# 16-head attention with the keys on the partitions: scores come transposed from the matmul, and VectorE casts the latent keys' exponentials

## The chip, the cores and the metric

The kernel runs on one core of one Trainium2 chip. A core has TensorE (PE in the profile, its weight loads PEld), VectorE (DVE), ScalarE (ACT), GpSimd (POOL) and SyncE (SP), which run their own queues and wait for each other through semaphores. SBUF is the working memory, PSUM (eight banks of 128 x 512 f32) takes what TensorE computes. The metric is the device time of one execution in microseconds (us); smaller is better.

## The reference

The program computes four residual blocks on x of 4 batches x 256 tokens x 128 channels. Only the third one is touched in its arithmetic:

```python
# first stage: gated mLSTM cross attention over ctx, second stage: 8-head attention with 5 experts, fourth: 8-expert MLP
x = x + jnp.tanh(g_xattn[1]) * _L1_xattn_ref(ctx_1024, mask_BxS2_bf1, _layernorm(x, axis=-1), ...)   # the third stage
...
def _L1_xattn_ref(features, masks, latents, gm, bm, gl, bl, Wq, Wk, Wv, Wo):     # HEADS = 16, DIM_HEAD = 64, b = 4
    x = _layernorm(features, gm, bm)              # 256 keys from the features
    lat = _layernorm(latents, gl, bl)             # 256 queries, and 256 more keys
    q = (lat @ Wq).reshape(b, q_len, HEADS, DIM_HEAD).transpose(0, 2, 1, 3)
    kv_input = jnp.concatenate([x, lat], axis=1)
    kv_mask = jnp.concatenate([masks, jnp.ones((b, q_len), dtype=bool)], axis=1)
    ...                                           # k, v = kv_input @ Wk, @ Wv; q = q * SCALE
    sim = jnp.einsum('bhqd,bhfd->bhqf', q, k)
    sim = sim - jax.lax.stop_gradient(jnp.max(sim, axis=-1, keepdims=True))
    sim = jnp.where(kv_mask, sim, -jnp.inf)
    alphas = jax.nn.softmax(sim, axis=-1)
    out = jnp.einsum('bhqf,bhfd->bhqd', alphas, v)
    return out.transpose(0, 2, 1, 3).reshape(b, q_len, INNER) @ Wo
```

## The kernel before

The four blocks run one after the other as four stages. Every product that matters is made in three f16 matmuls: each f32 operand is split into a high f16 half and a low f16 half (the rest), and high x high, high x low and low x high are accumulated (`three`, L949).

**The third stage** (`pe_c`, `act_c`, `dve_c`) works through 4 batches x 16 heads x 2 tiles of 128 queries, 128 units of one tile of scores, 128 queries x 512 keys. The work is software-pipelined by `step(b, t)`, written out by hand for 32 units of a batch, with the middle in a hardware loop; queues are in order, so this text sets the order of the work. A unit goes through these stations:

- `scores` (L977): three matmuls of 64 rows x 512 columns, queries on the partitions.
- DVE at L1196: one pass over the bank that adds the mask, writes the negated scaled scores `sm` to SBUF, and takes the row's minimum (the softmax maximum).
- ACT at L1109: exp of `sm` with that maximum as bias, to `Pr` (f32).
- PE at L1029: four f32 transposes, so that the keys come to the partitions, which the product with V needs.
- ACT at L1102 copies the transposed tile to f16 (`PTh`), DVE at L1204 subtracts it from the bank (`PTl`).
- PE at L1016 to L1018: 12 matmuls of 65 columns with V (the 65th column is one, it gives the denominator).
- DVE at L1214 and L1218, once for four units: reciprocal of the denominators, and the product.

Beside that run the projections (`project`: K and V in three matmuls of 512 columns, Q of 256; ACT copies the high half, L1089, DVE subtracts it, L1174), and for every batch four transposes of the attention's output (`turn_ao`) and two f32 output projections (`project_ao`, L998).

**The second stage** ends in `dve_b` with two normalisations of the latents (L685), ten products (L769), a sum, and the split of the latents (`latent_split`, L691 and L693); its queries' path is on DVE and PE. `split` (L1596, L1598) turns a chunk of 1024 weight columns into two f16 halves on POOL; before, the eight chunks of the fourth stage's weights are split in `pool_c`, in the first units of the third stage.

## Time and profile before

| | |
|---|---|
| median of 3 runs | 800.03 us (799.91 to 800.35) |
| span of the profiled execution | 798.0 us |
| busy share PE, DVE, ACT, POOL | 82%, 80%, 45%, 34% |
| third stage, 393.5 to 687 us | 293.5 us: PE busy 285.8, DVE 243.0, ACT 207.1, POOL 28.8 |
| end of the second stage, 353 to 393.5 us | 40.5 us: PE busy 16.3, DVE 31.1, ACT 7.7, POOL 10.1 |

The span runs from the first to the last instruction of the profiled execution; a run's time holds some 2 us more around it. A busy share is an average over stages that have different limits, so the stage's own rows count. In a timeline a row gives the start, the duration, and what ended the idle time before it; since instructions of one engine overlap, what a row of work costs in a dense stretch is the distance between two starts, not its duration.

### The profile page before, as it was taken

To read this page: it belongs to the slowest core of one execution; us is meant where nothing else is said; L and a number is where in the kernel's file an instruction comes from. 1 tells how busy PE (TensorE), PEld (TensorE's weight loads), DVE (VectorE), ACT (ScalarE), POOL (GpSimd) and SP (SyncE) were. 2 spreads that over 40 slices of the span, in tenths; PEclk is the share of its full clock that TensorE was granted. 3 is DMA by queue.
4 is the path that set the end of the run, shared out by engine and by line. 5 is a ranking of instruction groups with operands and counts; after the bars stand their busy time and mean duration, and the time that the engine had idled before them with its cause. 6 is when DMAs were issued, how large, how long until landed. Compare 5 with 4: busy or idle time off the path is not lost. (4 is left out here: it accounts for less than half of the span.)

```text
span 798.0 us, 16645 instructions
## 1 busy us (share of the span) xinstructions
PE 651.7 (82%) x5465; PEld 405.4 (51%) x5465; DVE 635.4 (80%) x1391; ACT 355.3 (45%) x657; POOL 272.4 (34%) x253
## 2 busy tenths in 40 slices
PE   6499757797488388472589999999999999889997
PEld 5376511443254154252245556655655665557675
DVE  5747899579869969959489887888688879478887
ACT  2432200421231141131257777677677757546652
POOL 4433355146537727664058000000000000046663
PEclk9999968689599689665599999999999999989999
DMA  6211000000000000020013000000000000000000
GB/s 200 67 33 54 28 0 0 1 1 1 0 1 0 0 0 0 0 79 0 1 40 95 1 2 2 1 0 0 0 0 0 0 1 2 1 1 0 0 0 27
DMA packets 13111, 12.75 MB, mean 16 GB/s; under 512 B 2080, under 2 KB 10896, under 8 KB 13072
## 3 DMA queue, kind: packets, MB, share of 16 engines
q1 hardware_dynamic: 13072, 12.25, 5.2%
q8 instruction: 22, 0.36, 0.2%
q14 instruction: 17, 0.14, 0.1%
HBM read 11.72 MB, written 0.52 MB: 15 GB/s over the span
## 5 line engine op out<-in xcount | busy, mean ns | idle before, releaser
L1632 PE MATMUL bank<-ident,work 128*128 128x128 f32 x788 | 127.5, 292 | 8.9 <-DVE work L1832 3.0
L1632 PEld LDWEIGHTS bank<-ident,work 128*128 128x128 f32 x788 | 98.2, 151 | 29.2 <-issue 6.2
L1204 DVE TENSOR_TENSOR PTl<-bank,PTh 128x512 f16<-128x512 f32 x128 | 87.7, 685 | 28.2 <-ACT PTh L1102 27.7
L1567 POOL TENSOR_SCALAR rs<-mv 128x2 f32<-128x2 f32 (+2 forms) x12 | 2.4, 198 | 311.6 <-DVE mv L1775 311.6
L1109 ACT ACTIVATE work<-sm,nm 128x512 f32<-128x512 f32 x128 | 92.0, 719 | 10.9 <-DVE nm L1196 9.7
L1196 DVE CUSTOM_DVE_ANT_0 sm<-bank,maskrow 128x512 f32<-128x512 f32 x128 | 87.2, 681 | 7.1 <-ACT work L1109 5.7
L711 DVE TENSOR_TENSOR work<-bank,gatev 128x512 f32<-128x512 f32 x120 | 79.0, 682 | 14.5 <-PE bank L464 14.1
L1102 ACT ACTIVATE PTh<-bank 128x512 f16<-128x512 f32 x128 | 76.1, 594 | 29.0 <-PE bank L1632 26.7
L462 PE MATMUL bank<-weights,xbTh 128*128 128x512 f16 x120 | 49.4, 412 | 29.1 <-DVE work L711 27.2
L1016 PEld LDWEIGHTS bank<-work,PTh 128*128 128x128 f16 x512 | 46.0, 97 | 52.8 <-issue 47.1
L1328 DVE TENSOR_TENSOR work<-work 128x512 f16<-128x512 f32 x64 | 57.1, 949 | 13.0 <-POOL work L1390 13.0
L1390 POOL TENSOR_SCALAR work<-work 128x512 f16<-128x512 f32 x64 | 53.0, 851 | 36.6 <-ACT work L1322 34.0
L1016 PE MATMUL bank<-work,PTh 128*128 128x65 f16 x512 | 61.2, 196 | 2.1 <-DVE PTl L1204 2.1
L1017 PE MATMUL bank<-work,PTh 128*128 128x65 f16 x512 | 60.2, 195 | 0.0
L487 PE MATMUL bank<-kTh,qTh 64*128 64x256 f16 x64 | 21.3, 347 | 47.5 <-ACT work L628 38.4
L1018 PE MATMUL bank<-work,PTl 128*128 128x65 f16 x512 | 59.6, 193 | 0.0
L628 ACT ACTIVATE work<-bank,nm 128x256 f32<-128x256 f32 x64 | 26.7, 472 | 63.0 <-DVE nm L736 63.0
L951 PE MATMUL bank<-k2h,q2h 64*128 64x512 f16 x128 | 49.5, 387 | 3.3 <-DVE q2l L1174 2.1
L839 POOL TENSOR_TENSOR work<-work 128x512 f32<-128x512 f32 x24 | 30.5, 1270 | 63.2 <-DVE work L711 60.9
L464 PE MATMUL bank<-weights,xbTl 128*128 128x512 f16 x120 | 49.3, 411 | 0.0
L463 PE MATMUL bank<-weights,xbTh 128*128 128x512 f16 x120 | 49.2, 410 | 0.0
L953 PE MATMUL bank<-k2h,q2l 64*128 64x512 f16 x128 | 48.2, 376 | 0.0
(269 smaller groups left out, 1804.7 us busy)
## 6 DMA issues: line engine op xcount, KB each, us to landing
stage<-in_L_ffn_w SPq DMA_DIRECT2D x8, 512.0 KB, 3.8
stage<-in_L_ffn_Wkv SPq DMA_DIRECT2D x4, 640.0 KB, 4.0
stage<-in_L_ffn_Wq SPq DMA_DIRECT2D x2, 640.0 KB, 4.8
xt<-in_x SPq DMA_DIRECT2D x1, 512.0 KB, 4.1
ct<-in_ctx SPq DMA_DIRECT2D x1, 512.0 KB, 5.4
wo<-in_L_xattn_Wo SPq DMA_DIRECT2D x1, 512.0 KB
stage<-in_L_xattn_Wv SPq DMA_DIRECT2D x1, 512.0 KB, 3.4
stage<-in_L_xattn_Wq SPq DMA_DIRECT2D x1, 512.0 KB, 3.4
```

Source lines behind the costliest of these rows:

```text
L711: dve.tensor_tensor(heads8(m.prod[:, k, e, :]), heads8(bank_pj[c % 2][:, :]), wide(g, DH1), ALU.mult).then_inc(s.prod_ready, 1)
L951: pe.matmul(o, ah, bh, start=True, stop=False)
L1016: pe.matmul(o, ph, vh, start=(j == 0), stop=False)
L1017: pe.matmul(o, ph, vl, start=False, stop=False)
L1018: ins = pe.matmul(o, pl, vh, start=False, stop=(j == KT - 1))
L1102: act.activation(m.PTh[:, u % 2, :, :].rearrange("p n c -> p (n c)"), bank_T[use % 2][:, :], ACT.Copy).then_inc(s.c_T_hi, 1)
L1109: act.activation(m.Pr[:, t % 2, :], m.sm[:, t % 2, :], ACT.Exp, scale=-1.0, bias=m.nm[:, t % 4, 0:1]).then_inc(s.c_exp_done, 1)
L1196: dve.tensor_tensor_reduce(m.sm[:, t % 2, :], bank_S[t % 2][:, :], m.maskrow[:, :], -(DH2 ** -0.5), 3e38, ALU.add, ALU.min, m.nm[:, t % 4, ...
L1204: dve.tensor_tensor(m.PTl[:, u % 2, :, :].rearrange("p n c -> p (n c)"), bank_T[use % 2][:, :], m.PTh[:, u % 2, :, :].rearrange("p n c -> ...
L1328: dve.tensor_tensor(m.hTl[:, a, f, :], m.hf[:, use % HR, :], m.hTh[:, a, f, :], ALU.subtract).then_inc(s.h_lo, 1)
L1390: pool.tensor_scalar(m.hTh[:, use // FT, use % FT, :], m.hf[:, use % HR, :], 1.0, 0.0, ALU.mult, ALU.add).then_inc(s.h_hi, 1)
L1632: return pe.transpose(dst, src, m.ident[0:src.shape[0], 0:src.shape[0]])
```

## The change

The third stage is written anew. A step now is a pair of heads with all 256 queries, 32 steps in all, in this order on PE (`step`): transposed scores of the feature keys (`scores_T(t, 0)`), the row maximum's scores for the next pair's first query tile (`row_max(t + 1, 0)`), a projection or a transpose (job c), transposed scores of the latent keys, `row_max(t + 1, 1)`, the K projection (job f), the product with V of the pair before (`values`), the V projection (job h).

- `scores_T` computes the scores with the keys on the partitions: per half 12 matmuls of 64 rows x 256 columns that alternate between the two heads (rows 0 to 63 and 64 to 127, and two banks), and then subtracts the row maxima by a product of ones with a diagonal matrix of the maxima (`diag`, bf16), two matmuls of 512 columns. The f32 transposes of the exponentials are gone.
- `row_max` computes the scores a second time, from the high halves alone, queries on the partitions, only for their maximum: two matmuls of 512 columns and two of 256 with the mask row. DVE takes the maximum of 1024 columns (`take_max`) and writes `diag` (`spread_max`), twice a step.
- ACT takes exp straight from the banks. For the two tiles of feature keys it does so twice, f32 (`Pf`) and f16 (`Ph`); for the latent keys once, f32, and DVE casts that to f16 (`high_latents`, 128 x 1024). POOL subtracts (`low_exps`).
- The maxima's banks are bk[6] and bk[7]; `values` writes bk[6] too, and `project_ao` bk[7].
- Four of the eight weight splits are moved from the third stage into the last batch of the second; the other four stay at the start of `pool_c`. `turn_ao`'s copies move from ACT to DVE. Names have moved: L1174 is now L1248 to L1253, L1214 and L1218 are L1281 and L1285, L1598 is L1708.

The core of the diff, lines added:

```diff
+                    for k in range(2):
+                        latent_rstd(k)
+                        split(N_W1 + 2 + k)
...
-            for n in range(N_W0, N_W1):
+            for n in range(N_W0, N_W1 + 2):
+                if n == N_W1:
+                    pool.wait_ge(s.pj_ready, B * X1)
...
+            def step(it, t):
+                jobs, b, n = c_jobs(t), t // HP2, t % HP2
+                scores_T(it, t, 0)
+                if t + 1 < STEPS_C:
+                    row_max(it, t + 1, 0)
+                if "c" in jobs:
+                    job(it, (t, "c"), jobs["c"])
+                scores_T(it, t, 1)
+                if t + 1 < STEPS_C:
+                    row_max(it, t + 1, 1)
+                if "f" in jobs:
+                    job(it, (t, "f"), jobs["f"])
+                if t >= 1:
+                    values(it, t - 1, t)
+                if b >= 1 and n in (2, 4):
+                    project_ao(it, n // 2 - 1, job_no[t - 1, "c"], bank_wo)
+                if "h" in jobs:
+                    job(it, (t, "h"), jobs["h"])
...
+            def row_max(it, p, i):
+                if i == 0:
+                    pe.wait_ge(s.c_pj_free, it * PJ + (k_no[p] + 1))
+                    pe.wait_ge(s.maskrow_ready, it + (p // HP2 + 1))
+                    if p >= 3:
+                        pe.wait_ge(s.c_O_free, it * HP2 + (p - 2))
+                    elif p >= 1:
+                        pe.wait_ge(s.c_max_done, 2 * p)
                 else:
+                    pe.wait_ge(s.c_max_done, it * PAIRS + (2 * p + 1))
+                for h in range(2):
+                    r = slice(DH2 * h, DH2 * h + DH2)
+                    pe.matmul(bank_rm[h][:, :], m.q2h[r, p % 4, i * P:(i + 1) * P], m.k2h[r, p % 2, :], start=True, stop=False)
+                for h in range(2):
+                    r = slice(DH2 * h, DH2 * h + DH2)
+                    ins = pe.matmul(bank_rm[h][:, 0:S], m.first_row[r, :], m.maskrow[r, :], start=False, stop=True)
+                ins.then_inc(s.c_M_ready, 1)
...
+            def scores_T(it, p, half):
+                if p >= 1:
+                    pe.wait_ge(s.c_exp_done, it * EXPS + (3 * (p - 1) + 2 + half))
+                pair = bank_kq[2 * half:2 * half + 2]
+                for k in range(2):
+                    kt = 2 * half + k
+                    for x in range(3):
+                        for h in range(2):
+                            r = slice(DH2 * h, DH2 * h + DH2)
+                            key = (m.k2h, m.k2l, m.k2h)[x][r, p % 2, kt * P:(kt + 1) * P]
+                            q = (m.q2h, m.q2h, m.q2l)[x][r, p % 4, :]
+                            pe.matmul(pair[h][:, k * S:(k + 1) * S], key, q, start=(k == 0 and x == 0), stop=False)
+                if half == 0:
+                    pe.wait_ge(s.c_D_ready, it * PAIRS + (2 * p + 2))
+                for h in range(2):
+                    less = m.diag[:, p % 2, h * S:(h + 1) * S].unsqueeze(1).to_broadcast([P, 2, S])
+                    ins = pe.matmul(pair[h][:, :].rearrange("p (k c) -> p k c", k=2), m.onesb[:, :], less, start=False, stop=True)
+                ins.then_inc(s.c_S_ready, 1)
...
+            def values(it, p, t):
+                pe.wait_ge(s.c_P_lo, it * EXPS + (3 * p + 3))
+                if t < STEPS_C - 1:
+                    pe.wait_ge(s.c_max_done, it * PAIRS + (2 * t + 4))
+                else:
+                    pe.wait_ge(s.c_O_free, p)
+                if p % 4 == 0:
+                    pe.wait_ge(s.c_pj_free, it * PJ + (v_no[p // 4] + 1))
+                for u in range(4):
+                    o = bank_out[:, u * (DH2 + 1):(u + 1) * (DH2 + 1)]
+                    head = 2 * (p % HP2) + u // 2
+                    for kt in range(KT):
+                        ph, pl = (x[:, p % 2, kt, u * P:(u + 1) * P] for x in (m.Ph, m.Pl))
+                        vh, vl = (v[:, kt, head, :] for v in (m.v2h, m.v2l))
+                        pe.matmul(o, ph, vh, start=(kt == 0), stop=False)
+                        pe.matmul(o, ph, vl, start=False, stop=False)
+                        ins = pe.matmul(o, pl, vh, start=False, stop=(kt == KT - 1))
+                ins.then_inc(s.c_O_ready, 1)
...
+            def exps(it, p, r):
+                act.wait_ge(s.c_S_ready, it * PAIRS + (2 * p + r // 2 + 1))
+                if p >= 1:
+                    act.wait_ge(s.c_P_lo, it * EXPS + (3 * (p - 1) + r + 1))
+                if r == 0 and p % HP2 == 0:
+                    act.wait_ge(s.maskbias_ready, it + (p // HP2 + 1))
+                if r < 2:
+                    src, bias = banks[:, 2:4, r * S:(r + 1) * S], m.maskbias[:, r:r + 1]
+                    hi, full = (a.rearrange("p (h c) -> p h c", h=2) for a in (m.Ph[:, p % 2, r, :], m.Pf[:, r, :]))
+                else:
+                    src, bias = banks[:, 4:6, :].rearrange("p h (k c) -> p h k c", k=2), 0.0
+                    full = m.Pf[:, 2:4, :].rearrange("p k (h c) -> p h k c", h=2)
+                if r == 2:
+                    act.activation(full, src, ACT.Exp, scale=DH2 ** -0.5, bias=bias).then_inc(s.c_exp_done, 1)
+                    return
+                act.activation(full, src, ACT.Exp, scale=DH2 ** -0.5, bias=bias)
+                act.activation(hi, src, ACT.Exp, scale=DH2 ** -0.5, bias=bias).then_inc(s.c_exp_done, 1)
...
+            def take_max(it, p, i):
+                dve.wait_ge(s.c_M_ready, it * PAIRS + (2 * p + i + 1))
+                dve.tensor_reduce(m.nmax[:, p % 2, i, :], banks[:, 6:8, :], AX.X, ALU.max, negate=True).then_inc(s.c_max_done, 1)
+            def spread_max(it, p, i):
+                dve.wait_ge(s.c_max_done, it * PAIRS + (2 * p + i + 1))
+                for h in range(2):
+                    at = (h * I + i) * P
+                    ins = dve.tensor_scalar(m.diag[:, p % 2, at:at + P], m.identb[:, :], m.nmax[:, p % 2, i, h:h + 1], None, ALU.mult)
+                ins.then_inc(s.c_D_ready, 1)
             def take_mask(b):
...
+            def high_latents(it, p):
+                dve.wait_ge(s.c_exp_done, it * EXPS + (3 * p + 3))
+                dve.tensor_copy(m.Ph[:, p % 2, 2:4, :], m.Pf[:, 2:4, :]).then_inc(s.c_P_hi, 1)
+            def step(it, t):
+                jobs, b, n = c_jobs(t), t // HP2, t % HP2
+                more = t + 1 < STEPS_C
+                if more:
+                    take_max(it, t + 1, 0)
+                    spread_max(it, t + 1, 0)
+                if "c" in jobs:
+                    low(it, (t, "c"), jobs["c"])
+                if more:
+                    take_max(it, t + 1, 1)
+                    if n == HP2 - 2 and t + 2 < STEPS_C:
+                        dve.wait_ge(s.c_max_done, it * PAIRS + (2 * t + 4))
+                        take_mask(it + (b + 1))
+                    spread_max(it, t + 1, 1)
+                if t >= 1:
+                    ins = take_out(it, t - 1)
+                    if b >= 1 and n in (2, 4):
+                        ins = add_x3(it, b - 1, n // 2 - 1, bank_wo)
                     ins.then_inc(s.c_O_free, 1)
+                high_latents(it, t)
+                for place in "fh":
+                    if place in jobs:
+                        low(it, (t, place), jobs[place])
...
+            def low_exps(it, p):
+                for r in range(3):
+                    kts = slice(r, r + 1) if r < 2 else slice(2, 4)
+                    if r < 2:
+                        pool.wait_ge(s.c_exp_done, it * EXPS + (3 * p + r + 1))
+                    else:
+                        pool.wait_ge(s.c_P_hi, it * HP2 + (p + 1))
+                    pool.tensor_tensor(m.Pl[:, p % 2, kts, :], m.Pf[:, kts, :], m.Ph[:, p % 2, kts, :], ALU.subtract).then_inc(s.c_P_lo, 1)
```

**DVE, one pair in the middle of a batch.** Before, more than two of the four units that make a pair of heads (sm is the pass for the maximum, PTl the low half of the transposed exponentials, work and k2l the low halves of V and K):

```order
L1196 ISA sm,nm<-bank,maskrow 128x512
L1196 ISA nm 128x1
L1174 TENSOR_TENSOR work<-bank,work 128x8x64
L1204 TENSOR_TENSOR PTl<-bank,PTh 128x512
L1196 ISA sm,nm<-bank,maskrow 128x512
L1196 ISA nm 128x1
L1174 TENSOR_TENSOR k2l<-bank,k2h 128x512
L1204 TENSOR_TENSOR PTl<-bank,PTh 128x512
L1196 ISA sm,nm<-bank,maskrow 128x512
L1196 ISA nm 128x1
L1174 TENSOR_TENSOR q2l<-bank,q2h 128x256
```

Now, the whole step (nmax the maxima, diag the diagonal matrix, CAST the f16 exponentials of the latent keys, the last two rows the low halves of K and V):

```order
L1259 TENSOR_REDUCE nmax<-banks 128x2
L1266 TENSOR_SCALAR diag<-identb,nmax 128x128 x2
L1253 TENSOR_TENSOR q2l<-banks,q2h 128x512
L1259 TENSOR_REDUCE nmax<-banks 128x2
L1266 TENSOR_SCALAR diag<-identb,nmax 128x128 x2
L1281 RECIPROCAL den<-banks 128x4
L1285 TENSOR_TENSOR work<-banks,den 128x2x64 x2
L1291 CAST attn<-work 128x1024
L1250 TENSOR_TENSOR k2l<-banks,k2h 128x512
L1248 TENSOR_TENSOR work<-banks,work 128x8x64
```

The eight passes for maximum and low half (L1196, L1204) have become two reductions, four small products and a cast; the reciprocal stands behind both reductions.

**PE, around the product with V.** Before (the unit's last V products, a V projection, four transposes, the next scores, the next V products):

```order
L1016 MATMUL bank<-work,PTh 128x65
L1017 MATMUL bank<-work,PTh 128x65
L1018 MATMUL bank<-work,PTl 128x65
L951 MATMUL bank<-wv1h,kvTh 128x512
L952 MATMUL bank<-wv1l,kvTh 128x512
L953 MATMUL bank<-wv1h,kvTl 128x512
L1632 MATMUL bank<-ident,work 128x128 x4
L951 MATMUL bank<-k2h,q2h 128x512
L952 MATMUL bank<-k2l,q2h 128x512
L953 MATMUL bank<-k2h,q2l 128x512
L1016 MATMUL bank<-work,PTh 128x65
```

Now (the subtraction of the maxima, the second `row_max`, the K projection, the first of the 48 V products):

```order
L1046 MATMUL banks<-diag,onesb 128x512 x2
L1023 MATMUL banks<-k2h,q2h 128x512 x2
L1026 MATMUL banks<-maskrow,first_row 128x256 x2
L956 MATMUL banks<-kvTh,wk1h 128x512
L957 MATMUL banks<-kvTl,wk1h 128x512
L958 MATMUL banks<-kvTh,wk1l 128x512
L1064 MATMUL banks<-work,attn 128x65
L1065 MATMUL banks<-work,attn 128x65
L1066 MATMUL banks<-work,attn 128x65
```

The V products, which followed the scores of another unit, now stand behind the maxima of the next pair; the four transposes have no counterpart.

**POOL, end of the second stage.** Before (wk1l the last of the second stage's weight chunks, rs the latents' reciprocal deviations, z the sum of the last output tile):

```order
L1598 TENSOR_TENSOR wk1l<-stage,wk1h 128x1024
L1567 TENSOR_SCALAR rs<-mv 128x6
L1568 TENSOR_TENSOR rs<-rs,mhalf 128x6
L1567 TENSOR_SCALAR rs<-mv 128x6
L1568 TENSOR_TENSOR rs<-rs,mhalf 128x6
L861 TENSOR_TENSOR work<-work 128x5x256
L862 TENSOR_TENSOR work<-work 128x5x128
L863 TENSOR_TENSOR z<-work 128x320
```

Now (L1706 and L1708 a weight chunk of the fourth stage):

```order
L1677 TENSOR_SCALAR rs<-mv 128x6
L1678 TENSOR_TENSOR rs<-rs,mhalf 128x6
L1706 TENSOR_SCALAR weights<-stage 128x1024
L1708 TENSOR_TENSOR weights<-stage,weights 128x1024
L1677 TENSOR_SCALAR rs<-mv 128x6
L1678 TENSOR_TENSOR rs<-rs,mhalf 128x6
L1706 TENSOR_SCALAR weights<-stage 128x1024
L1708 TENSOR_TENSOR weights<-stage,weights 128x1024
L874 TENSOR_TENSOR work<-work 128x5x256
L875 TENSOR_TENSOR work<-work 128x5x128
L876 TENSOR_TENSOR z<-work 128x320
L1379 MEMSET work 128x64
```

Behind each rs now stands a weight chunk ahead of z; two more stand ahead of the first rs, and four follow z's memsets directly.

## Rows read from the trace of the kernel before

**Rows 1.** Page of the profiled execution: its span.

```profile
span 798.0 us, 16645 instructions
```

**Rows 2.** Windows, one batch: PE, PEld, DVE, ACT, POOL busy, granted clock, DMA.

```profile
472.20:542.70 70.50, 70.50 (x718) 43.00 (x718) 57.67 (x146) 50.77 (x92) 0.00 (x0) 1.00 0.00 1
```

**Rows 3.** Timeline of PE in the third stage: start, duration, engine, line, operation.

```profile
641.48 0.60 PE L1632 MATMUL bank<-ident,work 128*128 128x128 f32 x4
642.01 0.39 PE L951 MATMUL bank<-k2h,q2h 64*128 64x512 f16 x1
...
642.76 0.20 PE L1016 MATMUL bank<-work,PTh 128*128 128x65 f16 x1
...
643.13 0.38 PE L951 MATMUL bank<-kvTh,wk1h 128*128 x1
...
643.78 0.60 PE L1632 MATMUL bank<-ident,work 128*128 128x128 f32 x4
```

**Rows 4.** Timeline of DVE in the third stage, columns as before.

```profile
419.52 0.17 DVE L1214 RECIPROCAL den<-bank 128x4 f32<-128x4 f32 x1
419.72 0.49 DVE L1218 TENSOR_TENSOR work<-bank,den 128x128 f32<-128x128 f32 x2
420.12 0.68 DVE L1196 CUSTOM_DVE_ANT_0 sm<-bank,maskrow 128x512 f32<-128x512 f32 x1
...
420.73 0.69 DVE L1174 TENSOR_TENSOR work<-bank,work 128x512 f16<-128x512 f32 x1
```

**Rows 5.** Timeline of PE, second stage: scores of heads 0 and 1, twelve matmuls.

```profile
145.45 0.39 PE L487 MATMUL bank<-kTh,qTh 64*128 64x256 f16 x1 [1.42 <-DVE kTl L724]
...
146.26 0.42 PE L489 MATMUL bank<-kTh,qTl 64*128 64x256 f16 x1
146.28 0.42 PE L488 MATMUL bank<-kTl,qTh 64*128 64x256 f16 x1
...
146.90 0.42 PE L489 MATMUL bank<-kTh,qTl 64*128 64x256 f16 x1
```

**Rows 6.** Windows, that stretch of the second stage, columns as in rows 2.

```profile
145.40:147.30 1.90, 1.85 (x12) 1.06 (x12) 1.55 (x3) 0.30 (x1) 0.00 (x0) 0.50 0.00 0
```

**Rows 7.** Groups by form and by line: DVE, ACT and POOL operations and their mean durations.

```profile
L1109 ACT ACTIVATE work<-sm,nm 128x512 f32<-128x512 f32 x128 | 92.0, 719 | 10.9 <-DVE nm L1196 9.7
...
L736 DVE TENSOR_REDUCE nm<-bank 128x2 f32<-128x512 f32 x32 | 21.7, 682 | 4.0 <-PE bank L489 3.5 <-issue 0.4
...
L1812 DVE CAST work<-work x2: 685/690/694, 19.8 to 21.9; 128x1024 f16<-128x1024 f32 x2
...
L1606 POOL TENSOR_TENSOR kvTl<-sm,kvTh x2: 1152/1576/2000, 23.2 to 25.9; 128x512 f16<-128x512 f32 x2
```

**Rows 8.** Timeline of POOL in the first units of the third stage.

```profile
409.95 1.05 POOL L1596 TENSOR_SCALAR weights<-stage 128x1024 f16<-128x1024 f32 x1
...
414.42 2.14 POOL L1598 TENSOR_TENSOR weights<-stage,weights 128x1024 f16<-128x1024 f32 x1
```

**Rows 9.** Timeline of DVE beside those two POOL operations.

```profile
410.09 1.24 DVE L685 TENSOR_SCALAR ct<-ct,mv,rs 128x128 f32<-128x128 f32 x2
...
415.88 0.96 DVE L693 TENSOR_TENSOR kvTl<-ct,kvTh 128x256 f16<-128x256 f32 x1 [0.48 <-ACT kvTh L667]
```

**Rows 10.** Timeline of DVE where the second stage ends and the third begins.

```profile
367.51 1.62 DVE L685 TENSOR_SCALAR ct<-ct,mv,rs 128x128 f32<-128x128 f32 x6 [0.16 <-POOL rs L1568]
...
384.44 0.42 DVE L693 TENSOR_TENSOR kvTl<-ct,kvTh 128x256 f16<-128x256 f32 x1 [0.48 <-ACT kvTh L667]
...
393.01 0.35 DVE L775 SCALAR_TENSOR_TENSOR xt<-bank,gf,xt 128x128 f32<-128x128 f32 x1 [3.06 <-PE bank L547]
...
402.20 0.69 DVE L1196 CUSTOM_DVE_ANT_0 sm<-bank,maskrow 128x512 f32<-128x512 f32 x1 [0.23 <-PE bank L953]
```

**Rows 11.** Timeline at the third stage's end: last normalisation, output projection.

```profile
686.89 0.18 DVE L1214 RECIPROCAL den<-bank 128x4 f32<-128x4 f32 x1 [0.64 <-PE bank L1018]
...
690.54 3.81 PE L998 MATMUL bank<-wo,work 128*128 128x128 f32 x32 [0.27 <-ACT work L1094]
```

567 lines of the change are left out of this document (274 added, 293 removed).

## The prediction

> **What bounds the kernel now.** I read the windows first. In a batch of the third stage PE is busy for the whole 70.50 us at a granted clock of 1.00, DVE for 57.67, ACT for 50.77, POOL not at all [rows 2]. So PE bounds it, at 70.5 / 8 = 8.81 us for two heads with 256 queries. The timeline of PE shows where that goes: four transposes .53 (641.48 to 642.01), three score matmuls with the changes between 64 and 128 rows .75, V products .37, a projection .65 (643.13 to 643.78) [rows 3]. Four units are 4 x 1.65 = 6.6; K .65, V .65 and half a Q projection .34 bring 8.24; the rest is the output's transposes and projections, a few times a batch. Whoever shortens PE's work gains until the next chain ends last, so the question is which chain that is.
>
> **The change: the work of each engine per step.** PE: a 512-column f16 matmul costs .65 / 3 = .22 at full clock [rows 3], 256 columns .11. The twelve matmuls of `scores_T` are 1.3 one behind the other. But they alternate between row groups, and in the second stage twelve such matmuls (256 columns, heads on different rows) begin within 146.90 - 145.45 = 1.45, in pairs .02 apart with .21 from pair to pair [rows 5], at a granted clock of .50 [rows 6], where one alone would take .22. Two run side by side. I take that: 6 x .11 = .66, .83 with the staggered ends that the second stage shows in proportion (1.66 / 2). The Trainium skill ("TensorEngine Tiling (Array Packing)", Key Properties) says that different tiles run in parallel and that a change of the tiling drains TensorE; the trace agrees on the first, and the second speaks for neither side, eight changes for a pair of heads before and now. So `scores_T` is .83 + 2 x .22 = 1.27 a half, 2.5 a step; two `row_max` at .35 are .7; jobs c, f, h .6, .65, .65; 48 V products 4 x .37 = 1.5 [rows 3]; changeovers some .4. Sum 7.0. PE alone would give 7.0 for 8.81.
>
> ACT: four exponentials and three copies of 512 columns or less at .72 or less and an exponential of 1024 at twice that, at most 6.5; POOL: 1.15 + 1.15 + 2.14 = 4.5, where a subtraction of 512 columns is 1.15 at least and one of 1024 is 2.14 [rows 7, 8]. Neither bounds.
>
> **The chain that I expect to end last** goes through DVE and bank 6, because row maxima and V products share it and the reciprocal stands behind both reductions. I follow it from the start of one first reduction to the next. Reduction of 1024 columns: 512 take .68 [rows 7], and dense rows stand .61 apart (420.12 to 420.73 [rows 4]), so 1.22. The two products for `diag`: no row has bf16; between .05 each (nothing but columns) and .27 (1.62 / 6, f32 [rows 10]), I take .21, as a row of 4 columns is .17 [rows 4]: .42. Low half of job c .61. Second reduction 1.22. Two hand-overs .08. Then PE: 48 V products and their last end, 1.5 + .2 = 1.7. Reciprocal and product .60 (419.52 to 420.12 [rows 4]), hand-over .07. The cast of 1024 columns .69 [rows 7], .61 in a row. Low half of K .69, which must be there before the next `row_max`. Hand-over .12, `row_max` with its last end .52. Sum 1.22 + .42 + .61 + 1.22 + .08 + 1.7 + .67 + .61 + .69 + .12 + .52 = **7.9**. PE, with 7.0 of work, waits for DVE and has gaps of about 1 us.
>
> **What POOL does to it.** In the trace of before, two products of 128 columns at 410.09 took 1.24 beside POOL's pass from 409.95 to 411.00, where six took 1.62 alone [rows 8, 9, 10]; and L693 at 415.88 took .96 beside POOL's 414.42 to 416.56, where it took .42 alone. Both ended just after POOL's did: a DVE operation whose operands lie in SBUF waits for the whole of POOL's. Now `low_exps` runs in each step. The 1024-column subtraction can start only when the cast is done, 1.9 - .6 = 1.3 before the next first reduction, and lasts 2.14, to .9 after; then the first 512-column one, whose exponentials are ready, to 2.05. The reduction reads PSUM and passes. The `diag` products (SBUF to SBUF) want to start at 1.25 and wait until 2.05: **+.75 a step**, 8.6 in all, on the path since the second reduction stands behind them on DVE, and the low half of c too. The bounds of this term: 0, if bf16 products aren't held or the subtractions fall elsewhere, and 1.15, a whole subtraction. I take the value of the order above. The Trainium skill ("SBUF — State Buffer", SBUF: two separate sides) says that VectorE and GpSimd share a port pair as an exclusive lock, taken by a DVE operation in a 2-port mode or with two SBUF inputs, and "VectorE: DVE Perf Modes" (What auto-detection actually checks) puts a single-source bf16 operation in SBUF into such a mode. By that rule the `diag` products and the cast are held, by its lack they are not: 8.6 against 7.9; the two rows above agree for f32.
>
> **Beside the steps.**
> - `project_ao` in six steps: 32 f32 matmuls take 3.81 [rows 11], so one projection 1.9, against PE gaps of which .4 hide it: +1.5 each, +9.
> - The first steps' normalisation of the latents, with its statistics and the last `lat` job on DVE: +4 (two operations of .6 and two of .5 in chains of three).
> - Entry. x is there at 393.36, and before reaches its first maximum at 402.20 [rows 10]. The new order has the same projections ahead of the same point but then two reductions with their products before step 0's: 402.2 + 2 x 1.64 = 405.5.
> - 31 steps x 8.6 = 266.
> - Exit, from the last first reduction on: second reduction and V products as above, the last pair's latent exponentials, cast (.61), subtraction (2.14), V products (1.7), reciprocal and product (.6): 8.5, some of it side by side with the scores; then transposes and their copy 1.6, less by two turned tiles than before: 10.1.
> - The end of the second stage, where four weight splits (1.05 + 2.14 each [rows 8]) now lie among DVE's SBUF work. One starts behind the first rs, while L685 wants to run six products in 1.62 [rows 10]: at worst they wait 3.2, I take +2.9. Four follow z directly (12.8 us of POOL); the latents' split on DVE (L693, .42 alone at 384.44 [rows 10]) and what hangs on it wait for pieces of it: between 0 and 6, I take +2.2. Together **+5.1**. What the splits leave in the third stage costs nothing there: PE bounded those units. Splits four to seven are needed only in the fourth stage.
> - The 1-byte mask loads and the other early DMAs are issued long before their use; they are hidden by the first two stages.
>
> Sum: 405.5 + 266 + 9 + 4 + 10.1 = 694.6 against the output projection's 690.5 before: +4.1, and +5.1 from the second stage: +9. The profiled execution's span of 798.0 [rows 1] becomes 807; the median of the runs is 2.0 above that span: 809, and rounded down for small covers **808**.
>
> **The rivals.**
> - *POOL does not hold DVE* (or not there). For: neither row is a bf16 operation, and POOL's order may drift until its passes lie beside the reductions. Then steps take 7.9, -31 x .75 = -23: **785**. The side changes at a hold of .48 a step. That is the case on the other side.
> - *The row groups do not run side by side* at full clock, or wait on other things. Each `scores_T` takes 1.3 + .43, +.45. PE's own chain (`row_max`, c, scores, `row_max`, wait for the maximum, V products, h, scores) then becomes the longest, 8.9 a step: +10, **819**; with `row_max` not in pairs either, up to 830. Against it stand rows 5.
> - *The clock falls*. PE is now busy for 7 of 8.6 us, with gaps of 1 us, and all rows of the third stage with a dense PE are at 1.00 [rows 2]; the second stage with gaps of 1.4 has .50 in a stretch [rows 5, 6]. If it fell for good, PE's 7 us would be near 13: beyond 900; for a third of the steps **850**.
> - *PE's saving comes through whole* (V products free of the second reduction by luck of order): 7.2 a step, 31 x 1.4 = 43 less, 765. Against it stands the wait in `values` for the second maximum.
>
> **How the numbers follow.** Forecast with a hold: .42. No hold, or half of it: .28, of which a tenth ends within .2%. Row groups or another wait on PE: .2. Clock: .04. PE alone: .06. What a measurement of this kernel can tell from no change is about .2%, 1.6 us. Faster, the second and last cases: .33; same, pieces of the first two: .07; slower: .60. The range takes in 785 and half of the third case: 782 to 832; the likeliest case's own is 799 to 817, from a hold of .45 to one of 1.0 a step.
>
> **What would show it.** In the profile after: the first reductions 8.6 apart; the `diag` products at 1 us and more for two, ending with POOL's subtraction; PE at some 82% of a batch at clock 1.00; `scores_T`'s matmuls in pairs .02 apart; L694 at the second stage's end at 4 us for six. The prediction is wrong if the `diag` products take .4 without a wait, if the matmuls stand .11 apart one by one, or if PE waits mostly for ACT's exponentials, for which my sums give no reason.

## The result

The changed kernel takes 839.8 us (median; 836.39 to 840.82), where the kernel before takes 799.97 in runs beside it: ratio 1.0486, 95% interval 1.0463 to 1.051, 5% slower. Forecast were 808 and a range of 782 to 832. The sign and the mechanism with the largest price (POOL holds the `diag` products) came true; the amount is five times the forecast, 39.8 us for 8.

The page of the changed kernel (span, busy per engine, and the granted clock in tenths over 40 slices):

```profile
span 839.1 us, 16283 instructions
...
PE 634.8 (76%) x5721; PEld 384.2 (46%) x5721; DVE 645.3 (77%) x1231; ACT 302.6 (36%) x533; POOL 413.5 (49%) x353
...
PEclk9999977597797598555699999999999998989998
```

Three milestones say where the 41.1 us of span went. x is ready for the third stage at 402.51 + .35 = 402.86 (393.36 before [rows 10]): +9.5. From there to the two output projections at 727.61 are 324.8 us (297.2 before [rows 10, 11]): +27.6. From there to the end 111.5 (107.5 before): +4.0.

```profile
402.51 0.35 DVE L787 SCALAR_TENSOR_TENSOR xt<-banks,gf,xt 128x128 f32<-128x128 f32 x1 [3.05 <-PE banks L556]
```

```profile
727.61 3.84 PE L1072 MATMUL banks<-wo,work 128*128 128x128 f32 x32 [0.34 <-DVE work L1238]
```

PE's first matmuls of a `scores_T` (x2 is one for each head):

```profile
564.53 0.28 PE L1041 MATMUL banks<-q2h,k2h 64*128 64x256 f16 x2
564.65 0.27 PE L1041 MATMUL banks<-q2h,k2l 64*128 64x256 f16 x2
564.76 0.27 PE L1041 MATMUL banks<-q2l,k2h 64*128 64x256 f16 x2
```

Timeline of DVE in two steps of a batch, one with a Q projection (first) and one with a transpose:

```profile
565.81 0.68 DVE L1248 TENSOR_TENSOR work<-banks,work 128x512 f16<-128x512 f32 x1
566.57 1.23 DVE L1259 TENSOR_REDUCE nmax<-banks 128x2 f32<-128x1024 f32 x1
567.83 1.01 DVE L1266 TENSOR_SCALAR diag<-identb,nmax 128x128 bf16<-128x128 bf16 x2
568.75 0.68 DVE L1253 TENSOR_TENSOR q2l<-banks,q2h 128x512 f16<-128x512 f32 x1
569.36 1.21 DVE L1259 TENSOR_REDUCE nmax<-banks 128x2 f32<-128x1024 f32 x1
570.60 0.42 DVE L1266 TENSOR_SCALAR diag<-identb,nmax 128x128 bf16<-128x128 bf16 x2
572.30 0.18 DVE L1281 RECIPROCAL den<-banks 128x4 f32<-128x4 f32 x1 [1.28 <-PE banks L1066]
...
574.87 1.23 DVE L1259 TENSOR_REDUCE nmax<-banks 128x2 f32<-128x1024 f32 x1
576.13 1.96 DVE L1266 TENSOR_SCALAR diag<-identb,nmax 128x128 bf16<-128x128 bf16 x2
578.01 0.68 DVE L1238 COPY work<-banks 128x512 f32<-128x512 f32 x1
578.61 1.21 DVE L1259 TENSOR_REDUCE nmax<-banks 128x2 f32<-128x1024 f32 x1
```

POOL beside it:

```profile
565.38 3.24 POOL L1391 TENSOR_TENSOR attn<-work,attn 128x1024 f16<-128x1024 f32 x2 [4.88 <-DVE attn L1291]
569.16 1.16 POOL L1391 TENSOR_TENSOR attn<-work,attn 128x512 f16<-128x512 f32 x1 [0.54 <-ACT attn L1169]
573.68 4.36 POOL L1391 TENSOR_TENSOR attn<-work,attn 128x1024 f16<-128x1024 f32 x3 [3.37 <-DVE attn L1291]
```

Two `diag` products take .42 where POOL is idle (570.60). At 567.83 they take 1.01 and end at 568.84, just after POOL's two subtractions (565.38 + 3.24 = 568.62). At 576.13 they take 1.96 and end just after POOL's three (573.68 + 4.36 = 578.04). Taken one by one, the two products of 576.13 and the passes of POOL that they meet are:

```profile
576.13 0.85 DVE L1266 TENSOR_SCALAR diag<-identb,nmax 128x128 bf16<-128x128 bf16 x1
576.90 1.19 DVE L1266 TENSOR_SCALAR diag<-identb,nmax 128x128 bf16<-128x128 bf16 x1
```

```profile
575.77 1.16 POOL L1391 TENSOR_TENSOR attn<-work,attn 128x512 f16<-128x512 f32 x1
576.89 1.16 POOL L1391 TENSOR_TENSOR attn<-work,attn 128x512 f16<-128x512 f32 x1
```

The first product waits for the rest of one pass and is done at 576.98, when that pass is (576.93). The second meets the next pass from its start and is done with it (578.09 and 578.05). At 567.83 only the first product is held, for .84, and the second runs in POOL's idle time. Of the 128 products in this execution 46 are held, each up to the end of one pass; none waits through two.

So an even step (with a Q projection) takes 574.87 - 566.57 = 8.30, and an odd one (with a transpose), from reciprocal to reciprocal, 9.25. PE waits for the second maximum. The groups of its waits between 393.5 and 728 us (total, times, longest):

```profile
PE banks L1064 <- DVE nmax L1259: 39.3, 27, 2.9
...
PE banks L1041 <- issue: 3.4, 2, 1.8
```

The reciprocals show three more kinds of step. After each of the six output projections inside the batches it takes 12.0 to 13.0 us from one reciprocal to the next. In batch 0 the intervals behind the latents' normalisation are 12.5 and 10.1. And in two of the six, where the hardware loop goes round, PE stands still for 1.6 and 1.8 us with nothing to wait for:

```profile
614.78 0.29 PE L1041 MATMUL banks<-q2h,k2h 64*128 64x256 f16 x2 [1.79 <-issue]
```

The granted clock of the third stage (420 to 726) is .95 where it was 1.00 in a batch before [rows 2]; behind an output projection it is less. A window of 12 us behind one (columns as in rows 2), and slices of 2 us behind a later one:

```profile
512.00:524.00 12.00, 9.97 (x109) 6.37 (x108) 8.07 (x14) 4.62 (x7) 4.44 (x3) 0.87 0.01 2
```

```profile
598.00:600.00 2.00, 0.85 (x19) 0.85 (x19) 1.51 (x3) 0.00 (x0) 0.00 (x0) 0.84 0.00 0
600.00:602.00 2.00, 2.00 (x35) 1.78 (x33) 0.12 (x1) 0.00 (x0) 0.00 (x0) 0.50 0.04 8
```

After a PE gap of 2.03 us (up to 599.15) the V products run at .50, the lower of the two levels, 1.2 GHz.

### The profile page after: what moved, and what is told of

It is laid out like the page before. It is cut to its first block, busy times and chain, and to the rows that moved or that the text cites. A ratio compares the mean times of both kernels' runs of the same rounds, so it can differ in the third digit from the quotient of the medians.

```text
span 839.1 us, 16283 instructions
## 1 busy us (share of the span) xinstructions
PE 634.8 (76%) x5721; PEld 384.2 (46%) x5721; DVE 645.3 (77%) x1231; ACT 302.6 (36%) x533; POOL 413.5 (49%) x353
## 4 chain that ended last, share of the span: by engine, by line
PE 42%; DVE 42%; issue 10%; POOL 3%; ACT 2%; DVEq 1%; DMA 1%; ACTq 0%; SPq 0%; POOLq 0%; PEld 0%
DVE nmax L1259 8%; DVE work L723 5%; DVE work L781 4%; PE banks L1746 3%; DVE diag L1266 3%; PE banks L1064 3%; PE banks L471 2%; PE banks L1066 2%; PE banks L1065 2%; PE banks L1452 2%; PE banks L1072 2%; PE banks L1453 2%; PE banks L1454 2%; PE banks L473 2%; PE banks L472 2%
## 5 line engine op out<-in xcount | busy, mean ns | idle before, releaser
L1391 POOL TENSOR_TENSOR attn<-work,attn 128x512 f16<-128x512 f32 (+1 forms) x96 | 141.0, 1481 | 170.3 <-DVE attn L1291 141.7
L1064 PE MATMUL banks<-work,attn 128*128 128x65 f16 x512 | 56.9, 203 | 47.4 <-DVE nmax L1259 39.3
L723 DVE TENSOR_TENSOR work<-banks,gatev 128x512 f32<-128x512 f32 x120 | 79.1, 682 | 15.5 <-PE banks L473 15.0
L1259 DVE TENSOR_REDUCE nmax<-banks 128x2 f32<-128x1024 f32 x64 | 77.7, 1215 | 10.8 <-PE banks L1026 9.4
L1064 PEld LDWEIGHTS banks<-work,attn 128*128 128x128 f16 x512 | 50.3, 104 | 62.1 <-DVE nmax L1259 45.6
L471 PE MATMUL banks<-weights,xbTh 128*128 128x512 f16 x120 | 50.6, 422 | 27.8 <-DVE work L723 26.4
L1266 DVE TENSOR_SCALAR diag<-identb,nmax 128x128 bf16<-128x128 bf16 x128 | 59.5, 506 | 2.2
L1746 PE MATMUL banks<-ident,work 128*128 128x128 f32 x276 | 53.3, 331 | 8.6 <-DVE work L1946 3.0
L1168 ACT ACTIVATE work<-banks,maskbias 128x512 f32<-128x512 f32 x64 | 44.0, 688 | 39.8 <-PE banks L1046 36.4
L1066 PE MATMUL banks<-work,attn 128*128 128x65 f16 x512 | 56.9, 203 | 0.0
L1065 PE MATMUL banks<-work,attn 128*128 128x65 f16 x512 | 56.8, 203 | 0.0
L1066 PEld LDWEIGHTS banks<-work,attn 128*128 128x128 f16 x512 | 50.9, 104 | 0.0
L1065 PEld LDWEIGHTS banks<-work,attn 128*128 128x128 f16 x512 | 50.7, 104 | 0.0
L1452 PE MATMUL banks<-weights,work 128*128 (+1 forms) x256 | 47.7, 229 | 2.9 <-DVEq L1502 2.9
L472 PE MATMUL banks<-weights,xbTh 128*128 128x512 f16 x120 | 49.9, 416 | 0.0
L473 PE MATMUL banks<-weights,xbTl 128*128 128x512 f16 x120 | 49.8, 415 | 0.0
```

What stands on the lines that cost most here:

```text
L471: pe.matmul(o, xh, wh, start=True, stop=False)
L472: pe.matmul(o, xh, wl, start=False, stop=False)
L473: pe.matmul(o, xl, wh, start=False, stop=True).then_inc(s.pj_ready, 1)
L723: dve.tensor_tensor(heads8(m.prod[:, k, e, :]), heads8(bank_pj[c % 2][:, :]), wide(g, DH1), ALU.mult).then_inc(s.prod_ready, 1)
L1064: pe.matmul(o, ph, vh, start=(kt == 0), stop=False)
L1065: pe.matmul(o, ph, vl, start=False, stop=False)
```

## The experiments

Each is the changed kernel with the edit named, unless it says otherwise. Medians in us; the ratio is against the kernel before, run beside it on the same chip. Medians of the kernel before differed by up to .65% from one such group of runs to the next (799.97 to 805.16), so a difference of under 4 us between kernels of different groups says little. The last two columns are read from the profiled execution: when x is ready for the third stage, and how long it takes from there to the output projections. x ready differs by up to 10 us between kernels with the same second stage (see e1), so the third stage's own time is the better measure of an edit in it.

| run | edit | median | ratio, 95% interval | x ready | third stage |
|---|---|---|---|---|---|
| kernel before | | 799.97 | | 393.4 | 297.2 |
| changed kernel | | 839.8 | 1.0486 (1.0463 to 1.051) | 402.9 | 324.8 |
| e1 | splits back behind z | 834.41 | 1.0388 (1.0284 to 1.0492) | 394.1 | 326.9 |
| e2 | POOL's short subtractions nearly left out | 803.44 | 1.0013 (.9972 to 1.0054) | 402.6 | 289.8 |
| e3 | `diag` products late | 808.74 | 1.0073 (1.0028 to 1.0119) | 407.6 | 293.4 |
| e4 | PE repeats K | 843.5 | 1.0475 (1.0386 to 1.0565) | 403.2 | 327.9 |
| g1 | kernel before, splits early | 808.73 | 1.0076 (1.0036 to 1.0116) | 399.1 | 297.0 |
| f1 | e3 and splits back | 804.29 | 1.0031 (.9989 to 1.0072) | 395.1 | 297.0 |
| f2 | e3 and ACT for the cast | 799.25 | .9944 (.99 to .9988) | 398.5 | 286.3 |
| f4 | e3 and loop written out | 802.29 | 1.0002 (.9964 to 1.004) | 398.6 | 288.4 |
| h1 | ACT for the cast alone | 825.61 | 1.0262 (1.0196 to 1.0327) | 400.5 | 312.4 |
| h3 | e3, ACT, loop written out | 796.44 | .992 (.9883 to .9956) | 398.3 | 281.0 |
| h2 | h3 and splits back | 792.52 | .988 (.9837 to .9923) | 404.0 | 283.0 |
| i1 | e4 and loop written out | 829.9 | 1.0375 (1.029 to 1.046) | 398.1 | 317.2 |

**e2: POOL's short subtractions.** My theory was that POOL's passes hold the `diag` products and, through them, the second reduction; the rival, that the clock costs most.

```diff
-                    pool.tensor_tensor(m.Pl[:, p % 2, kts, :], m.Pf[:, kts, :], m.Ph[:, p % 2, kts, :], ALU.subtract).then_inc(s.c_P_lo, 1)
+                    cs = slice(0, 16) if r < 2 else slice(None)
+                    pool.tensor_tensor(m.Pl[:, p % 2, kts, cs], m.Pf[:, kts, cs], m.Ph[:, p % 2, kts, cs], ALU.subtract).then_inc(s.c_P_lo, 1)
```

> POOL subtracts only 16 of 512 columns for the two tiles of feature keys (the rest of these low halves is left out); the semaphores and the 1024-column subtraction stay. Theory (POOL's passes hold the diag products, and through them the second reduction): a step with a Q job takes 8.3 us and can lose 0.25 before PE's second row_max is late instead, a step with a transpose takes 9.25 and can lose 1.35. With 15 and 14 of them and the first steps, 20 to 28 us faster, near 815; diag products 0.42 for two, except where the 1024-column subtraction lies beside them. Rival (the clock's fall costs most): the waits shrink, but steps at half clock stay, gain under 10 us.

It gave 36.4 us, more than the 20 to 28 expected. The plain steps inside the batches take 7.86 to 8.03, those behind an output projection 9.5 (11.2 and 11.4 where the loop goes round), where they took 12.0 to 13.0. One line of the `diag` products over the run (min, median, max in ns), none of which is held now:

```profile
L1266 DVE TENSOR_SCALAR diag<-identb,nmax x128: 246/250/266, 409.1 to 675.2; 128x128 bf16<-128x128 bf16 x128
```

**e3: the same products elsewhere.** e2 leaves work out; this edit leaves none out and lets POOL work as before.

```diff
                     take_max(it, t + 1, 0)
-                    spread_max(it, t + 1, 0)
...
                     take_max(it, t + 1, 1)
+                    spread_max(it, t + 1, 0)
                     spread_max(it, t + 1, 1)
```

> The products for the first diag come behind the second reduction instead of between the two; nothing is left out. Only the next step's scores need them. Theory (the hold costs because the second reduction stands behind the held products): the four products (0.84 together) fit into DVE's wait of 1.3 us for the V products, and POOL's two subtractions end about when the second reduction does, so the gain is that of the short subtractions within 5 us: 18 to 28 us faster. Rival (DVE's work is the bound wherever the products stand, or the hold only moves to behind the second reduction): under 8 us.

31.1 us, somewhat more than the range of 18 to 28. The timeline of DVE (an odd step, from reduction to reciprocal):

```profile
563.71 1.23 DVE L1259 TENSOR_REDUCE nmax<-banks 128x2 f32<-128x1024 f32 x1
564.85 0.68 DVE L1238 COPY work<-banks 128x512 f32<-128x512 f32 x1
566.03 1.22 DVE L1259 TENSOR_REDUCE nmax<-banks 128x2 f32<-128x1024 f32 x1 [0.50 <-PE banks L1026]
567.17 0.73 DVE L1266 TENSOR_SCALAR diag<-identb,nmax 128x128 bf16<-128x128 bf16 x4
568.99 0.18 DVE L1281 RECIPROCAL den<-banks 128x4 f32<-128x4 f32 x1 [1.09 <-PE banks L1066]
```

POOL's three subtractions still lie here (562.52 to 566.88), but nothing of DVE's wants SBUF alone before 567.17. Now the second reduction waits .50 for PE. PE's row of work (V products, V projection, scores, `row_max`) ends last, with a wait of .57 for the second maximum (1.88 in a plain odd step of the changed kernel, at 562.33). And the clock over a batch is up:

```profile
480.00:560.00 80.00, 71.73 (x921) 39.06 (x918) 59.53 (x127) 46.26 (x74) 41.70 (x29) 1.00 0.01 2
```

e2 and e3 take the hold away in two independent ways, and the plain steps and those behind a projection become the same in both. So the hold on the `diag` products, with the second reduction queued behind them, is shown as the main cause: the third stage is some 35 us (e2) and 31 us (e3) shorter. In both it then takes less than in the kernel before (289.8 and 293.4 for 297.2); what keeps them behind it lies in the second and the fourth stage.

**e4 and i1: the clock.** PE repeats the K projection's three matmuls in its gap, once more in even steps and three times more in odd ones.

```diff
-                    ins = three(pe, bank[:, :], m.wk1h[:, w], ...)
+                    for again in range(1 if place[0] < 0 else 2 if place[0] % 2 == 0 else 4):
+                        ins = three(pe, bank[:, :], m.wk1h[:, w], ...)
```

> PE repeats the K projection's three matmuls in each step, once more in even steps and three times more in odd ones, in the gap ahead of the V products where it waits for the second maximum (0.85 us in even, 2.0 us in odd steps); the result is the same. Theory (the clock falls in steps with long PE gaps and costs 1.0 to 1.3 us there, in some nine places of the third stage): the granted clock of the third stage goes to 0.98 or more and the kernel gets 7 to 12 us faster although PE does 40 us more work. Rival (the clock costs little, the holds are the whole loss): within 3 us of 839.8, or slower by what no longer fits the gaps.

Forecast missed: 843.5, no gain. But the steps show two effects that cancel. Behind four of the output projections a step takes 11.0 in place of 12.0 to 12.2, and the clock behind them is 1.00 in place of .87:

```profile
512.00:524.00 12.00, 11.91 (x156) 7.50 (x153) 8.20 (x14) 4.62 (x7) 4.45 (x3) 1.00 0.01 2
```

At the two places where the loop goes round, a step took 17.6 and 16.5 (12.8 and 13.0 without the repeats). PE has idle times in which it waits for no one:

```profile
536.49 0.28 PE L1042 MATMUL banks<-q2h,k2h 64*128 64x256 f16 x2 [1.63 <-issue]
...
539.46 0.37 PE L1042 MATMUL banks<-q2h,k2h 64*128 64x256 f16 x1 [2.36 <-issue]
```

i1 is the same kernel with the third stage's hardware loop written out.

```diff
-            with pe.Fori(0, B - 1) as it:
-                for t in range(SPLIT_AT, SPLIT_AT + HP2):
+            for it in (0,):
+                for t in range(SPLIT_AT, SPLIT_AT + (B - 1) * HP2):
```

> The repeated K projection of the earlier run, with the third stage's loop written out as well; the diag products stay between the reductions, and the result is the same. Theory (the repeats did keep the clock up and gave 1.0 to 1.2 us in four steps after an output projection, but the longer program let PE's instructions come late where the loop goes round, 5 us more at each of two places): without the loop those two steps also take 11.0, and the kernel comes to 827 to 832, some 10 us under the changed kernel, of which 4 to 5 are the clock's. Rival (instructions come late for another reason): two steps of 16 to 17 us stay, near 840.

829.9, inside the expected range, but x is ready 4.8 us earlier in its trace, which this edit doesn't explain; the third stage is some 7.5 us shorter, and the steps behind all six projections are at 10.7 to 11.0. The clock over the third stage is .98:

```profile
421.00:726.00 305.00, 277.81 (x3265) 155.51 (x3264) 235.61 (x441) 151.37 (x237) 139.45 (x101) 0.98 0.01 2
```

So the fallen clock costs 1.0 to 1.2 us in each of the four steps behind a projection. At the two where the loop goes round it falls later, from 544.7 on in the first of them, and costs 1.4 in the step that follows (9.70 and 9.74, where e4 has 8.29 and 8.30). That makes some 7 us inside the batches, and it is a consequence of the hold: in e3 the steps behind four of the projections take 9.5 at full clock. Plain steps that don't follow such a step never lost clock.

**f4: the loop's turn.** e3 with the same loop edit.

> The diag products late, and the third stage's hardware loop over three batches is written out step by step on each engine; the work is the same. Theory (PE's idle times of 1.4 to 2.0 us that end with nothing but issue, in the steps where the loop goes round, are instructions that come late): they are gone, 2 x 1.9 = 4 us less than 808.7. Rival (they come from something else in those steps): they stay at the same steps, same time; or the longer program brings others.

6.4 us less than e3, where 4 were expected (the ratios differ by .7%, the third stages by 5.0 us). PE has no idle time left that ends with issue in these steps; the steps at the two places take 9.56, where e3 had 11.44 and 13.12. The 13.12 holds more idle time and lower clock than the 1.4 and 2.0 us of issue alone. In before, PE had no such row in the third stage. Why the instructions come late in the changed loop is open: e4's longer loop made it worse (up to 2.65 us), and that the loop's text decides is all that these runs show.

**e1, g1 and f1: the four weight splits.** e1 puts them back behind z (three places of `pool_b` and `pool_c`), f1 does so with e3, and g1 makes only this part of the change in the kernel before.

```diff
                         latent_rstd(k)
-                        split(N_W1 + 2 + k)
...
-            for n in range(N_W0, N_W1 + 2):
-                if n == N_W1:
-                    pool.wait_ge(s.pj_ready, B * X1)
+            for n in range(N_W0, N_W1):
...
-            for n in range(N_W1 + N_EARLY, N_WALL):
+            for n in range(N_W1, N_WALL):
```

> The four weight splits that the change moved into the second stage go back behind z, eight in a row there; nothing else changes. Theory (POOL's passes hold DVE's operations in SBUF): in the trace after, the two groups of six L694 took 2.66 and 4.06 us where they take 1.62 alone, so 3.5 us come back at the second stage's end; the eight splits then last 25.6 us behind z and hold a few diag products of the third stage's first steps, about 1 to 3 us. Sum: 0.5 to 3 us faster than 839.8. Rival (the second stage lost its 9.5 us to the clock, not to the splits): no change within 1.5 us.

> The kernel before, with one part of the change alone: the four weight splits moved into the second stage's last batch, at the same places. Theory (they hold DVE's products there, and PE's clock falls with the waits): x is ready 6 to 9 us later than at 393.4, and nothing comes back in the third stage, which PE bounds: ratio 1.007 to 1.011. Rival (the second stage's delay in the changed kernel came from the clock or another part of the change): within 0.2% of before.

> The diag products late, as in the run before, and the four splits back behind z. Theory: the splits cost 8.7 us of the second stage, and in the third the later diag products have slack to absorb eight splits behind z; against 808.7 with late products alone it gives 5 to 9 us, so 800 to 804. Rival (what the second stage gains is lost again in the first steps, as with the splits put back alone, where 5.4 of 8.7 us came through): 5 us or less.

g1 is 1.0076 of before, inside the expected range: this part alone costs some 6 us (3 to 9 by the interval), and the third stage gives nothing back. Its timeline shows the hold on f32 products, the two groups of six that took 1.62 alone [rows 10]:

```profile
364.16 2.65 DVE L685 TENSOR_SCALAR ct<-xt,mv,rs 128x128 f32<-128x128 f32 x6
...
370.82 4.06 DVE L685 TENSOR_SCALAR ct<-ct,mv,rs 128x128 f32<-128x128 f32 x6 [0.16 <-POOL rs L1570]
```

x is ready at 399.11 there. In e1 x is ready at 394.1, 8.7 us earlier than in the changed kernel, and the kernel gained 5.4 where .5 to 3 were expected. Only 3.5 of the 8.7 are the holds on L694, as expected: from the first L694 to x it takes 32.9 in place of 36.3. The other 5.2 lie ahead of that row, where the edit changes nothing. f2's second stage is the changed kernel's to the letter, but its row begins where that of before and that of e1 do (361.88 and 361.27). The row in the changed kernel, then in f2:

```profile
366.52 2.66 DVE L694 TENSOR_SCALAR ct<-xt,mv,rs 128x128 f32<-128x128 f32 x6
```

```profile
361.38 3.44 DVE L694 TENSOR_SCALAR ct<-xt,mv,rs 128x128 f32<-128x128 f32 x6
```

f4, h1, h3 and i1, with the same second stage too, have it at 361.0 to 362.8, but e2 and e4 at 366.3 and 366.9 and e3 at 371.3, and h2, with the splits back, at 371.2. What differs is the granted clock ahead of it. The changed kernel, then f2, between 280 and 290 us:

```profile
280.00:290.00 10.00, 9.37 (x60) 6.86 (x58) 2.42 (x4) 3.61 (x11) 0.00 (x0) 0.56 0.00 0
```

```profile
280.00:290.00 10.00, 8.62 (x68) 6.29 (x68) 3.65 (x7) 3.91 (x12) 0.00 (x0) 0.81 0.00 0
```

So 4.6 of the 9.5 us that the changed kernel loses up to x are no price of the splits. What makes the clock fall in one trace and not in another with the same work is open. The splits' own price is 4.9: 3.5 at L694, and 1.4 at two rows L705 (.91 and 1.32 for .42), which e1 keeps, since splits follow z directly there too. g1's 5.8 divide in the same way, 2.3 ahead of the first group and 3.4 behind its start.

In the traces 5.2 of e1's 8.7 reach the end: its third stage is 2.1 us longer and its fourth 1.4. f1's 4.4 fall under its range of 5 to 9 and within what two groups of runs can tell; the rival's bound holds. Its third stage is 3.6 us longer than e3's, 1.9 of that up to the third reciprocal, as the rival had it.

**f2 and h1: the cast on ACT.** The piece of the change that its title names, undone.

```diff
-                if r == 2:
-                    act.activation(full, src, ACT.Exp, scale=DH2 ** -0.5, bias=bias).then_inc(s.c_exp_done, 1)
-                    return
+                    hi = m.Ph[:, p % 2, 2:4, :].rearrange("p k (h c) -> p h k c", h=2)
...
-                high_latents(it, t)
```

POOL's subtraction then waits for ACT in place of the cast.

> The diag products late, and ACT makes the f16 exponentials of the latent keys too (a second Exp of 1024 columns), so the cast on DVE is gone; nothing is left out. Theory (with the products late, PE's own row of work ends last: from V products to the next row_max it never waits, except about 0.1 for K's low half): only some 0.1 to 0.2 us of the 0.6 a step come through, so 3 to 6 us less than 808.7. Rival (DVE's chain still bounds the step): 0.5 us or more a step, 15 to 19 us less.

> The changed kernel with one edit: ACT makes the f16 exponentials of the latent keys (a second Exp of 1024 columns) in place of the cast on DVE; the diag products stay between the reductions. Theory (the cast costs mostly through POOL: it lets the 1024-column subtraction start late, which pushes the 512-column ones together onto the diag products in odd steps): the subtraction of 1024 columns starts ahead of the reciprocal, odd steps go from 9.25 to about 8.3, even ones stay, and with the steps after an output projection this gives 12 to 20 us, so 820 to 828. Rival (the cast costs only its own time on DVE, and PE's row_max then ends last): 3 to 6 us.

f2 is 9.5 us under e3 (ratios 1.3% apart), between the two theories' ranges; its third stage is 7.1 shorter. Its reciprocals give the parts: the 27 intervals from the second reciprocal on are 2.4 us shorter together, some .1 each (.2 in most plain steps), as expected where PE ends last, and the last three are 3.7 us shorter. The rest of the 7.1 lies in the first intervals; what of the 9.5 lies outside that stage isn't shown to be the edit's. h1 came to 825.6 inside its range, but for another reason than the one I wrote, so that was luck. Most of its odd steps still take 9.1 to 9.2, and their products are still held, though the 1024-column subtraction is long done. The timelines of POOL and DVE of h1:

```profile
563.88 2.13 POOL L1385 TENSOR_TENSOR attn<-work,attn 128x1024 f16<-128x1024 f32 x1 [0.68 <-ACT attn L1167]
568.52 2.31 POOL L1385 TENSOR_TENSOR attn<-work,attn 128x512 f16<-128x512 f32 x2 [2.51 <-ACT attn L1167]
```

```profile
568.87 2.01 DVE L1264 TENSOR_SCALAR diag<-identb,nmax 128x128 bf16<-128x128 bf16 x2
```

In an odd step ACT has no Q copy between the two tiles of feature keys, so the second exponentials are there when the first subtraction ends, and two of 1.15 follow each other without a gap; in an even step there is a gap of some .5 in which DVE gets in. So the odd steps' longer hold doesn't come from the cast. h1's gain lies in the last two intervals (4.5 and 4.5 us for 8.6 and 6.4), 5.0 in the 27 intervals before them, 2.5 in the first two, and x ready 2.3 us earlier, which isn't the edit's.

**h3 and h2: what adds up.** h3 is e3 with ACT's exponentials and the loop written out; h2 puts the splits back as well.

> Diag products late, latent f16 exponentials on ACT, and the loop written out; the splits stay in the second stage. Theory (the three act on different things, and their gains of 31.1, 9.5 and 6.4 us add up): 839.8 less 47 is 793, 1.0% under before. Rival (the written-out program and the exponentials on ACT give the same waits back): 799 or more.

> The same with the four splits back behind z. Theory: 4 to 5 us less than with three, about 788, 1.5% under before. Rival (eight splits behind z hold back the first steps' subtractions on POOL, for which the V products wait): the same as with three within 2 us.

h3's 796.4 lies between the two, short of the full sum (793) by 3.4; h2's 792.5 is 1.2% under before, where 788 and 1.5% were expected, and with overlapping intervals it isn't told apart from h3. In both the odd steps are at 8.38 and the even ones at 7.4: in the odd ones the last of the four late products now meets the earlier subtraction of 1024 columns and takes 2.13, the other three run before it. h2's timeline:

```profile
545.63 2.61 DVE L1261 TENSOR_SCALAR diag<-identb,nmax 128x128 bf16<-128x128 bf16 x4
```

So part of the gain is given back there. Both are faster than the kernel before by about 1%, with intervals that end below 1, as f2's does at .6%.

## Why the prediction was wrong

- **PE's work and the side-by-side row groups** (right). `scores_T`'s matmuls start in pairs .11 apart at full clock (564.53 for the first two, 564.65 for the next), .76 from the first start to that of the product with `diag`, where I had .83. The rival of single matmuls is out.
- **The chain through DVE and bank 6** (right). Without holds it is 7.9 to 8.0 by e2 and e3, and 7.9 by my sum. Which link ends last is another: PE's work behind the V products, not the cast and K's low half. The cast is worth .1 to .2 a step, not .6 (f2).
- **POOL's hold** (right mechanism, wrong size). In even steps the products wait .59 (1.01 for .42), a step is 8.30 where I had 8.6. I took every step for the same. In odd steps the hold is 1.5 and the step 9.25: the subtractions of both tiles follow each other, since no Q copy of ACT's lies between, and the second product meets a pass of its own. My upper bound of 1.15, "a whole subtraction", is the bound for one product; there are two (.6 and .9 us of wait in the rows at 576.13, and both with a whole pass, 2.32 in all, in the first steps). By the Trainium skill ("SBUF — State Buffer", SBUF: two separate sides) the one that comes second is blocked for the whole of the other's instruction; the rows agree, one pass for each product.
- **The output projections inside the batches** (the step that failed most). I put +1.5 on each for PE's work alone. e2 and e3 show just that, 9.5 against 8.0. In the changed kernel the steps behind them take 12.0 to 13.0, against 10.1 by my sums, about 14 us in all, and 2 more in the steps right behind. They are odd steps with the long hold (+.7 over my step); the V products behind PE's gap of 2.03 us run at half clock (1.0 to 1.2, e4); and in two, PE's instructions come late (1.6 and 1.8). I had reckoned with PE gaps of about 1 us and priced a falling clock as a rival of its own, not as a cost in the steps with the longest wait.
- **The first steps**: 12.5 and 10.1 against +4 over two steps of 8.6, 1.4 too little; the products beside rs and two subtractions took 2.32.
- **The third stage's end**: from the last first reduction (704.80) to the output projections (727.61) it takes 22.8, where the sum has the last step and 10.1, 18.7 in all. I priced the last V products at 1.7 (full clock). PE waits 3.35 us for POOL's last subtraction ahead of them, and they take 2.9 (722.50 to the reciprocal at 725.36) at a granted clock of .57:

```profile
722.50 0.24 PE L1064 MATMUL banks<-work,attn 128*128 128x65 f16 x1 [3.35 <-POOL attn L1391]
```

- **The second stage's end**: +9.5 against +5.1. The term for the splits was right, 4.9 (L694 2.66 and 4.06 for 1.62, L705 .91 and 1.32 for .42). The other 4.6 are PE's clock ahead of them, and no price of the change: f2, f4, h1, h3 and i1, with the same second stage, don't have them.
- **The fourth stage**: +4.0, where I had nothing. Its granted clock is .94 for .96, with the same work (PE 101.4 us busy for 97.8). g1, in which it starts late too, takes 107.5 (clock .96); f2, in which it starts 5.7 us earlier than in before, takes 111.6. So a late start isn't the reason. No run settles what lowers the clock there; it stays open.

Together: 4.4 (second stage) + 23.6 (third: 324.8 for the forecast's 301.2) + 4.0 (fourth) make the 32 us by which the span of 839.1 passes the 807 of the sum. Of the 23.6, about 16 are those of the output projections, 4 the stage's end, 3 the plain steps (+.65 in odd, -.3 in even ones) and 1.4 the first ones. The hold alone doesn't explain the miss: without any hold I had 785, and e2 without holds takes 803.4.

## What to carry to other kernels

Before pricing a hold between POOL and DVE, write down what ACT and POOL do in each kind of step: a DVE operation that is held waits for one pass of POOL's, but where passes follow each other without a gap the next operation meets the next pass, so count the products as well as the passes. A cheap product held is dear when a reduction that TensorE waits for stands behind it. Placing it behind that reduction gave back 31 us here with no work saved. Price TensorE's clock in the steps with the longest gap, not in the mean; here, where the wait was made shorter, the clock came back with it. And before a difference of a few us is put down to an edit, look whether it lies in a stretch that the edit touches.

## What was not expected of the hardware

- A DVE operation in SBUF on bf16 (128 columns, .25 alone) is held by POOL's subtraction just as f32 ones are, up to the end of one pass: .85 and 1.19 for two in a row, the second behind the next pass. A gap of .54 us between passes was enough for the second to run free (.24).
- Behind a PE gap of 2.03 us the clock was at half for some 3 us. In the plain odd steps a gap of nearly the same length (1.88 us, at 562.33) left it at 1.00; which of the differences between these steps decides wasn't tried.
- PE stood still for 1.2 to 2.7 us with nothing but issue where a hardware loop goes round, for longer in all with the longer loop, and not at all once it was written out.
- The granted clock in one and the same stretch of work (280 to 290 us) was .50, .56 and .81 in the traces of e3, the changed kernel and f2, whose second stage is the same; that moved the end of the stretch by up to 10 us.
